# A graph network's sorting stage: ScalarE makes 12 of the 31 columns of each target one-hot, and VectorE compares with numbers held in PSUM

## The reference

```
x = _layernorm(x + _L0_gnn_ref(x, edge_attr_128, src, dst, ...))   # segment_sum(edge_attr, dst), then an MLP
x = _layernorm(x + _L1_gnn_ref(x, edge_index, ...))                # attention over edges, softmax over all of them
x = _layernorm(x + _L2_gnn_ref(x, edge_index, ...))                # edge MLP on x[src], x[dst], segment_sum by dst
x = _layernorm(x + _L3_gnn_ref(x, edge_index, ...))                # normalised sum of neighbours, then a matrix
```

## Time and profile before

| | |
|---|---|
| three runs | 6006.87, 6010.56, 6012.87 us, median 6010.56 |
| profiled execution | 6002.25 us, its span 6000.4 us |
| the stage `edge_sums_and_lists` | about 105 to 816 us of the span |
| busy over the span | PE 91%, PE weight load 81%, DVE 74%, ACT 33%, POOL 22% |
| mean granted TensorE clock | 0.968 over the span, 1.00 in the stage |

### The profile page before, as it was taken

How to read it: one execution, slowest core, us unless ns; L and a number is a source line. 1 busy time by engine, 2 the same in 40 slices (tenths; PEclk the granted TensorE clock), 3 DMA queues, 4 the chain that set the end, 5 groups by cost and what they waited for, 6 DMA issues and landing times. The chain is left out here.

```text
span 6000.4 us, 165282 instructions
## 1 busy us (share of the span) xinstructions
PE 5460.5 (91%) x58225; PEld 4831.4 (81%) x58310; DVE 4419.3 (74%) x7547; ACT 1966.0 (33%) x4615; POOL 1340.5 (22%) x1304
## 2 busy tenths in 40 slices
PE   2999989799999999999977699999999997699986
PEld 2888877799999999999965499999999996466655
DVE  7999952688888888888864467777777773388874
ACT  0000024344444444344433222222222222266641
POOL 1444446333333333333323300000000001200000
PEclk9999999999999999999989899999999997899988
DMA  6444422222222222222211133333333330100000
GB/s 115 156 158 151 151 71 71 98 96 90 95 90 95 90 90 92 95 91 94 90 42 37 43 123 116 122 117 120 116 120 116 118 119 18 58 0 0 0 1 23
DMA packets 206210, 523.66 MB, mean 87 GB/s; under 512 B 33555, under 2 KB 85398, under 8 KB 199318
## 3 DMA queue, kind: packets, MB, share of 16 engines
q1 hardware_dynamic: 195936, 518.35, 25.5%
q10 hardware_dynamic: 10179, 4.02, 0.3%
HBM read 485.12 MB, written 37.19 MB: 87 GB/s over the span
## 5 line engine op out<-in xcount | busy, mean ns | idle before, releaser
L1281 PE MATMUL ps<-kv_table,stage 128*128 128x256 bf16 x7644 | 1251.9, 273 | 28.9 <-DVE stage L1137 27.3
L1669 PE MATMUL ps<-a_table,stage 128*128 128x128 bf16 x7644 | 843.5, 219 | 31.3 <-DVE stage L1552 31.3
L1672 PE MATMUL ps<-window,stage 128*128 128x128 bf16 x7800 | 861.1, 219 | 0.0
L1284 PE MATMUL ps<-window,stage 128*128 128x128 bf16 x7800 | 860.3, 219 | 0.0
L1206 ACT ACTIVATE q_kept<-ps 128x512 f32<-128x512 f32 (+1 forms) x676 | 392.8, 581 | 1156.9 <-PE ps L1284 1156.9
L1571 DVE TENSOR_TENSOR slot_hot<-iota,slots 128x512 f32<-128x512 f32 (+1 forms) x676 | 454.1, 672 | 412.2 <-PE ps L1684 401.7
L1622 ACT ACTIVATE edge<-ps 128x512 f32<-128x512 f32 x624 | 374.0, 599 | 1105.3 <-PE ps L1684 1068.4
L1281 PEld LDWEIGHTS ps<-kv_table,stage 128*128 128x128 bf16 x7644 | 668.2, 98 | 70.1 <-issue 27.9
L1253 POOL TENSOR_TENSOR message<-message 128x512 f32<-128x512 f32 (+1 forms) x468 | 482.5, 1031 | 985.7 <-ACT message L1215 985.7
L1284 PEld LDWEIGHTS ps<-window,stage 128*128 128x128 bf16 x7800 | 654.5, 98 | 59.1
L1684 PE MATMUL ps<-edge,slot_hot 128*128 128x130 f32 x4992 | 697.1, 282 | 0.0
(11 more groups left out here) (340 smaller groups left out, 8350.3 us busy)
## 6 DMA issues: line engine op xcount, KB each, us to landing
stage<-lists SPq DMA_DIRECT2D x312, 768.0 KB, 4.1
edges<-in_edge_attr SPq DMA_DIRECT2D x52, 1984.0 KB, 7.7
stage<-lists SPq DMA_DIRECT2D x104, 896.0 KB, 5.4
window<-qkv_rows SPq DMA_DIRECT2D x52, 288.0 KB, 4.7
qkv_rows<-kv_table SPq DMA_DIRECT2D x26, 384.0 KB, 2.5
window<-ab_rows SPq DMA_DIRECT2D x52, 192.0 KB, 4.3
qkv_rows<-q_parts SPq DMA_DIRECT2D x26, 192.0 KB, 2.0
ab_rows<-a_table SPq DMA_DIRECT2D x26, 192.0 KB, 2.0
```

What stands on the lines that cost most here:

```text
L1281: nc.tensor.matmul(kv_ps[n % 2][:, i, :], from_src, kv_table[:, tile, q, :], start=(q == 0), stop=(q == 2))
L1284: last = nc.tensor.matmul(q_ps[n % 2][:, i, :], own, window[d][:, q * D:(q + 1) * D], start=(q == 0), stop=(q == 2))
L1669: nc.tensor.matmul(edge_ps[n % 2][:, i, :], from_src, a_table[:, tile, q, :], start=(q == 0), stop=False)
L1672: last = nc.tensor.matmul(edge_ps[n % 2][:, i, :], own, window[d][:, (3 + q) * D:(4 + q) * D], start=False, stop=(q == 2))
```

## The change

ACT makes the columns 19 to 30 of each `dst_hot`, DVE only the columns 0 to 18 (`SHARE = 19`). A column on ACT is one instruction: `Abs(rel - number)` over 128 numbers, with a bias of one number per edge. When the twelve are done, one `Relu(1 - value)` over all 1536 elements turns 0 into 1 and all greater values into 0. ACT does this between `vals(j+1)` and the copy of the totals (j+1).

The rows of numbers that DVE compares with now lie in PSUM: PE writes `iota` and `iota1` into bank 2 once, by a product with the identity, and both `dst_hot` and `bucket_hot` read them there. Since TOTALS was in bank 2, it moves to bank 7, where CODES and TURNED are; `totals_step` then also waits for the copy of TURNED (`turned_sb`). `sum_step` also waits for ACT's columns (`hot_act0`).

```diff
+        IOTA_PS = ps[:, 2, P:2 * P]
+        IOTA1_PS = ps[:, 2, 2 * P:3 * P]
-        TOTALS = ps[0:G, 2, 0:BUCKETS]
+        TOTALS = ps[0:G, 7, 2 * P:2 * P + BUCKETS]
...
-            return dve.tensor_tensor(hot[:, 0:G, :], over_chunks(iota1[:, 0:BUCKETS], G), over_columns(ids, BUCKETS),
+            return dve.tensor_tensor(hot[:, 0:G, :], over_chunks(numbers[:, 0:BUCKETS], G), over_columns(ids, BUCKETS),
                                      ALU.is_equal)
...
+            SHARE = 19
+            hot_act0 = sem("hot_act0")
+            apart0 = sem("apart0")
...
+                    def target_step(j, g, b):
+                        act.wait_ge(summed0, j + 1)
+                        for c in range(SHARE, G):
+                            last = act.activation(dst_hot[b][:, c, :], iota, ACT.Abs, bias=of_group(rel, g)[:, c:c + 1],
+                                                  scale=-1.0)
+                        last.then_inc(apart0, 1)
+                        act.wait_ge(apart0, j + 1)
+                        act.activation(dst_hot[b][:, SHARE:G, :], dst_hot[b][:, SHARE:G, :], ACT.Relu, bias=ones[:, 0:1],
+                                       scale=-1.0).then_inc(hot_act0, 1)
...
                         act.activation(vals[0][:, 0, :], of_group(dr1, 0), ACT.Copy)
                         act.activation(vals[0][:, 1, :], of_group(lo1, 0), ACT.Copy).then_inc(vals_kept, 1)
+                        target_step(first * 2, 0, 0)
                         totals_step(first * 2)
...
                                 vals_step(j + 1, g + 1, d)
+                                target_step(j + 1, g + 1, d)
                                 totals_step(j + 1)
...
                     def target_step(j, g, b):
                         dve.wait_ge(summed0, j + 1)
-                        dve.tensor_tensor(dst_hot[b][:, :, :], over_chunks(iota, G), over_columns(of_group(rel, g), P),
-                                          ALU.is_equal).then_inc(hot0, 1)
+                        dve.tensor_tensor(dst_hot[b][:, 0:SHARE, :], over_chunks(IOTA_PS, SHARE),
+                                          over_columns(of_group(rel, g)[:, 0:SHARE], P), ALU.is_equal).then_inc(hot0, 1)
...
+                    nc.tensor.matmul(IOTA_PS, ident, iota, start=True, stop=True)
+                    nc.tensor.matmul(IOTA1_PS, ident, iota1[:, :], start=True, stop=True).then_inc(iota_set, 1)
...
                     def totals_step(j, b):
                         pe.wait_ge(bucketed, j + 1)
                         pe.wait_ge(totals_sb, j + 1)
+                        pe.wait_ge(turned_sb, j)
...
                         pe.wait_ge(hot0, j + 1)
+                        pe.wait_ge(hot_act0, j + 1)
```

More of the change, by code:

```diff
@@ L358, in gnn_program @@
         moved = sem("moved")
-        TOTALS = ps[0:G, 2, 0:BUCKETS]
+        iota_set = sem("iota_set")
+        IOTA_PS = ps[:, 2, P:2 * P]
+        IOTA1_PS = ps[:, 2, 2 * P:3 * P]
+        TOTALS = ps[0:G, 7, 2 * P:2 * P + BUCKETS]
         PREFIX = ps[:, 3:7, 0:8 * BUCKETS]
@@ L364, in gnn_program, with buckets_dve @@
         assert GP == 32 and 8 * BUCKETS <= 512 and 2 * TILES <= P
-        def buckets_dve(dve, hot, ids):
-            return dve.tensor_tensor(hot[:, 0:G, :], over_chunks(iota1[:, 0:BUCKETS], G), over_columns(ids, BUCKETS),
+        def buckets_dve(dve, hot, ids, numbers):
+            return dve.tensor_tensor(hot[:, 0:G, :], over_chunks(numbers[:, 0:BUCKETS], G), over_columns(ids, BUCKETS),
                                      ALU.is_equal)
@@ L509, in _ @@
                         act.activation(vals[0][:, 1, :], of_group(lo1, 0), ACT.Copy).then_inc(vals_kept, 1)
+                        target_step(first * 2, 0, 0)
                         totals_step(first * 2)
                         vals_step(first * 2 + 1, 1, 1)
+                        target_step(first * 2 + 1, 1, 1)
                         totals_step(first * 2 + 1)
@@ L538, in _ @@
                     dve.wait_ge(moved0, MOVE + 5)
+                    dve.wait_ge(iota_set, 1)
                     dve.sem_inc(moved, 1)
@@ L542, in bucket_step @@
                         dve.wait_ge(paid, j)
-                        buckets_dve(dve, bucket_hot[b], of_group(bucket, g)).then_inc(bucketed, 1)
+                        buckets_dve(dve, bucket_hot[b], of_group(bucket, g), IOTA1_PS).then_inc(bucketed, 1)
                     def target_step(j, g, b):
                         dve.wait_ge(summed0, j + 1)
-                        dve.tensor_tensor(dst_hot[b][:, :, :], over_chunks(iota, G), over_columns(of_group(rel, g), P),
-                                          ALU.is_equal).then_inc(hot0, 1)
+                        dve.tensor_tensor(dst_hot[b][:, 0:SHARE, :], over_chunks(IOTA_PS, SHARE),
+                                          over_columns(of_group(rel, g)[:, 0:SHARE], P), ALU.is_equal).then_inc(hot0, 1)
                     def rank_step(j, g, b, ahead):
@@ L571, in _ @@
                         dve.wait_ge(paid, first * 2 + 1)
-                        buckets_dve(dve, bucket_hot[0], of_group(bucket, 0)).then_inc(bucketed, 1)
+                        buckets_dve(dve, bucket_hot[0], of_group(bucket, 0), IOTA1_PS).then_inc(bucketed, 1)
                         target_step(first * 2, 0, 0)
@@ L634, in _ @@
                     with pe.Fori(0, total, PAIRS) as first:
+                        pe.wait_ge(turned_sb, first * 2 + 1)
                         totals_step(first * 2, 0)
@@ L887, in resort_dve @@
                 after(5)
-                buckets_dve(dve, r["hot"], r["bucket"]).then_inc(step, 1)
+                buckets_dve(dve, r["hot"], r["bucket"], iota1[:, :]).then_inc(step, 1)
                 after(9)
```

## The result

The changed kernel takes 5992.65 us in the median of 12 runs (5984.93 to 6001.35), the kernel before 6010.02 (12 runs, 6004.59 to 6015.22): 17.4 us less, a ratio of 0.9971, 95% interval 0.9964 to 0.9979. Forecast were 5987.5 (range 5980 to 5996) and 23 us. The profiled execution has 5992.28 us, span 5990.4.

A forecast was written before the change was run, and what follows sets the result against it. DVE, 99% busy, was taken to bound the stage, PE close behind. Steps -28.0, semaphores +1.0, ACT's start +3.3 and PE's slow start +0.5 give -23.2 us: forecast 5987.5, range 5980 to 5996.

The forecast's parts named there:

- PE's wait for `dst_hot`: Before the sum in each step: 29.1 us of PE idle time, the most a faster `dst_hot` can return.
- Sum 1 to sum 51: The 50 steps of the loop: 50 x 0.56 = 28.0 us gained, less 1.0 for added semaphore waits.
- A step on PE alone: Loop step without the wait, read from step 1: 12.84 us against 13.40, so 0.56 gained a step.
- a further semaphore: PE's two added waits, on semaphores set long before: 0.02 us taken, 1 us in all.
- rival 2: DVE stays the bound as the standing moves from `bucket_hot` to `rank_hot`: no change, or 0.4 saved a step, 5995; chance 0.08.
- 1.5 to spare: ACT between second `vals` and the copy of the totals: 5.3 us of work in a 6.8 window, so hidden.
- Rival 1: ACT late at the copy of the totals, ahead of PE's prefixes: 28 us slower, 6039; chance 0.10, mild form 0.04 more.
- turning point of 0.46 a column: ACT's time for each of its twelve columns at which the change turns from faster to slower.
- a rule against this division: Skill's rule that relu-like work is VectorE's, up to three times as fast; rows said to agree: 1.60 us against 5.3.
- The start: Step 0, where nothing hides ACT: totals copied 3.3 us later, plus 0.5 for PE's slow first microseconds.
- The other term, 0.5 for a longer slow start of PE: PE's first sum: a longer pause may lengthen its slow start by up to 1.2 us; 0.5 taken.
- Nothing later depends on the change: Everything behind the stage's loop: claimed to take the same time, a term of 0.

The follow-up runs named there:

- e1: Changed kernel with DVE making all 31 columns and ACT none, numbers still in PSUM: 5979.67 us, ratio to the kernel before 0.9947.
- e6: e1 with one more semaphore ahead of each sum, given by ACT a whole step earlier: 5983.09 us, ratio to the kernel before 0.9958.
- e5: e1 with dst_hot's numbers back in SBUF, so only bucket_hot's lie in PSUM: 5983.45 us, ratio to the kernel before 0.9959.
- e7: Changed kernel with 20 instead of 12 columns on ACT: 6114.42 us, ratio to the kernel before 1.0171.
- e3: Changed kernel with step 0's one-hot made by DVE alone: 5986.96 us, ratio to the kernel before 0.9963.
- e2: Changed kernel with ACT's 12 columns kept, numbers in SBUF and TOTALS in bank 2 as before: 5989.22 us, ratio to the kernel before 0.9959.

## Why the prediction was right, and where its sizes were off

**The bound and the wait.** Right. PE's wait for `dst_hot` was the thing to gain, and nothing took its place: no row of the changed kernel shows PE waiting for DVE or ACT before a sum. Sum 1 to sum 51 fell by 26.7 us, forecast 27.0. That it is so close is luck: small errors cancel. A step on PE alone is 12.80, not 12.84 (e1; the step read in the earlier trace rows was of the longer kind of two that alternate), and a further semaphore costs 0.05, not 0.02 (e6); 0.5 more went in one step behind ACT's slow store.

**DVE.** `dst_hot` 2.68 forecast and 2.68 measured, `bucket_hot` 1.77 and 1.76, `rank_hot` 3.5 to 4.5 and 4.01. The standing did move from `bucket_hot` to `rank_hot`, as the prediction and rival 2 both say; that it would cost the gain, as in rival 2, did not come: `pay` is first in each step, and its end plus 2.15 fixes DVE's chain with time to spare. POOL can be the one that stands, too, though not behind `rank_hot`: before, the first instruction of `pay` started at 462.01, while `dst_hot` ran (458.50 to 462.78), and took 3.41 us; in the changed kernel, where they do not meet, it takes 2.78. What the prediction did not draw from its own argument is that with this slack the columns need not leave DVE: from `pay`'s end `dst_hot` with 31 columns would end 1.6 later and still be in time. e1 and e5 show it.

**ACT.** Columns spaced 0.29 forecast, (3.62 - 0.39) / 11 = 0.29 measured; `Relu` 1.57 and 1.58; 1.5 to spare and 1.69. The register instruction ahead of each column was hidden: the twelve take 3.62 in the loop and 3.60 in step 0, which has none. Rival 1's place is right: what ACT has too much comes on top of each step (e7: 14.54, worked out from the changed kernel's rows as 14.5). Its turning point of 0.46 a column was not reached in any run, and its price leaves out what a longer wait on PE can do to the clock.

The prediction also sets a rule against this division and says that the rows agree on its ratio. They do not bear on it: the Trainium skill ("ScalarE: Activation LUTs", "Rules for kernel authors") gives "up to about 3×" for bf16 operations with one source, and here float32 is compared with two operands. For one more element a pass takes 0.84 ns on ACT (0.387 us for 128, 1.58 for 1536) and 1.04 on DVE (2.68 for 2432, 4.28 for 3968). ACT needs 5.2 us against DVE's 1.60 because it makes two passes and pays a fixed part for each of its instructions.

**The start.** 3.8 forecast; 3.0 against the mean of three profiles, 2.8 against e3. The mechanism was right: the totals are copied 5.23 us after the second `vals` instead of 2.09, 3.1 later (3.3 forecast). The other term, 0.5 for a longer slow start of PE, did not come. Sum 0 takes 8.91 in the changed kernel and 8.39, 9.31 and 9.50 before; without it the start is 15.4 in all three profiles before and 18.5 now, the same 3.1.

**The end: the step that failed.** It is "Nothing later depends on the change", together with 50 steps taken whole. The stretch from sum 51 to the first product behind the stage got 3.3 us longer. Sum 51 and the transpose ahead of it stand behind PE's loop. In all ten profiles the products of that sum stop with nothing waited for ("issue"), and go on 3.5 to 4.2 us after the start of that transpose: 3.85, 3.54 and 3.85 before, 4.19 changed, 3.62, 3.61, 3.66, 3.71, 4.16 and 3.72 in e1, e2, e3, e5, e6, e7. An earlier start of the sum only makes the stop longer, so the last half microsecond is not gained. Against the first profile before, the 3.2 us are 0.5 of this, 0.3 for the longer distance (4.19 instead of 3.85), 0.7 because 51 instead of 46 products are left, and 1.6 because these 51 take 7.59 us instead of 5.96 (e3).

That last part is clock. In e1, e2, e3 and e5 (stops of 1.74, 1.40, 1.89 and 1.61) it stays at 1.00 behind the stop, and the stretch takes 18.7 to 19.3. In the changed kernel, e6 and e7 (stops of 2.43, 2.39 and 1.91) the granted clock is 0.60, 0.68 and 0.57 over the next 4 us, and the stretch takes 21.0 to 21.5. The length of the stop alone does not decide it: in e7's stage waits of 1.68 and 1.78 were followed by a low clock, in e3 a stop of 1.89 was not. The changed kernel, busy times in short stretches:

```profile
782.00:786.00 4.00, 3.91 (x21) 3.91 (x22) 0.75 (x1) 0.00 (x0) 3.39 (x1) 0.60 0.02 4
786.00:790.00 4.00, 4.00 (x43) 4.00 (x43) 0.18 (x1) 0.00 (x0) 0.00 (x0) 0.97 0.00 0
```

That the stop is the loading of PE's next instructions is my reading of "issue" and of the nearly constant distance (3.5 to 4.2) from the first transpose behind the loop; no run changed the length of that code, so it is argued, not shown, and the cause of the stop stays open. Nor is it settled whether the longer of the two forms comes in every execution of the changed kernel.

The remaining 3 us, from the stage's -20.4 to -17.4 in the medians, lie inside the interval (-12.6 to -21.6 us). Whether the code behind the stage takes the same time is open: 5184.1 to 5189.2 us in the three profiles before, 5186.5 to 5194.5 in the seven others (one of each kernel), 4.5 more in the mean.

## What to carry to other kernels

When one engine waits half a microsecond in each step for another that is 99% busy, the gain is that half microsecond and no more (0.56 a step here): read the step in which the wait is missing, and count how little it takes to reach it. Here two independent cures were applied, each enough alone; one of them (moving the operand of one VectorE comparison into PSUM, so that it no longer stands behind GpSimd) cost nothing that shows (e5), and the other brought a longer start, a further semaphore in each step and a ScalarE with 1.7 us left of the 6.9 between `vals` and the totals. The versions without ScalarE's columns beat both kernels: 5979.7 us (e1) and 5983.5 (e5) against 5992.7 and 6010.0.

## What the runs showed of the hardware that was not expected

- A semaphore that has long been set costs PE 0.05 us a step as the fourth that the sum waits for (e1 12.80, e6 12.85). As the third that the totals wait for (`turned_sb`) it costs nothing that shows: 12.86 a step without it (e2) and with it (the changed kernel).
- A wait of 1.7 to 2.0 us on PE can be followed by a granted clock of 0.50 (1.2 GHz), so that it costs more than itself: in e7 0.67 us a step on top of 1.68, by the difference.
- Behind the end of this loop PE's products stop until 3.5 to 4.2 us after the start of the first transpose there (ten profiles), whether the sum started 0.8 us after that transpose or 0.3.
- In every run the VectorE instruction that stood behind GpSimd's was the one with both operands in SBUF that started while `pay` ran: `bucket_hot` 3.18 and `rank_hot` 2.28 before, 1.76 and 4.01 after, 4.28 and 2.28 with the columns moved alone (e2). `chosen` (one operand in PSUM) and the rank (one operand) took 1.81 to 1.83 and 1.82 throughout. An operand in PSUM costs VectorE nothing that shows: 2432 elements take 2.68 us with the numbers in PSUM (changed) or in SBUF (e2).
